# Third expert layer of a decoder: token parts of 12, 12 and 8 tiles in place of 8, 12 and 12, with the first part's scatters sent four at a time

## What is computed

```
def _L3_ffn_ref(x, keys, w1, b1, w2, b2, rw, rb):
    E, TOP_K = (16, 4)
    diff = x[:, :, None, :] - keys
    dist2 = jnp.sum(diff * diff, axis=-1)
    logits = -dist2 + jnp.einsum('bld,ed->ble', x, rw) + rb
    topv, topi = jax.lax.top_k(logits, TOP_K)
    w = jax.nn.softmax(topv, axis=-1)
    hidden = jax.nn.gelu(jnp.einsum('bld,efd->blef', x, w1) + b1, approximate=False)
    exp_out = jnp.einsum('blef,edf->bled', hidden, w2) + b2
    sel = jnp.take_along_axis(exp_out, topi[..., None], axis=2)
    fused = jnp.sum(w[..., None] * sel, axis=2)
    return fused
...
    x = _layernorm(x + _L3_xattn_ref(x, ctx_512, ...), axis=-1)
    x = _layernorm(x + _L3_ffn_ref(x, L3_ffn_keys, ...), axis=-1)
```

## Time and profile before

| what | value |
|---|---|
| median of 3 runs | 4205.87 us (4192.5 to 4210.88) |
| the profiled execution: its time | 4187.43 us |
| its span, first to last instruction | 4185.6 us |
| mean granted TensorE clock | 0.868 of full speed |
| PE busy | 3230.9 us, 77% of the span |
| DVE, ACT, POOL busy | 2781.3, 2066.4, 1179.1 us |

### The profile page before, as it was taken

How to read it: one execution, slowest core, us unless ns; L and a number is a source line. 1 busy time by engine, 2 the same in 40 slices (tenths; PEclk the granted TensorE clock), 3 DMA queues, 4 the chain that set the end, 5 groups by cost and what they waited for, 6 DMA issues and landing times. The chain is left out here.

```text
span 4185.6 us, 91928 instructions
## 1 busy us (share of the span) xinstructions
PE 3230.9 (77%) x33262; PEld 2232.8 (53%) x33262; DVE 2781.3 (66%) x7659; ACT 2066.4 (49%) x4648; POOL 1179.1 (28%) x2276
## 2 busy tenths in 40 slices
PE   6886888796888776857898989668865588779881
PEld 2443555463555446854555555345544456569881
DVE  5884677374787584547787888577754668844453
ACT  3664666223443543535786878445640344346551
POOL 2322221012110233451111111253312520334555
PEclk9987999697998687977999999688985699889996
DMA  4424331033220431231212121423430500222332
GB/s 94 67 34 61 57 53 36 16 98 50 32 38 11 62 69 57 79 69 35 50 27 42 36 38 30 67 35 65 60 79 11 172 20 1 77 68 88 90 84 62
DMA packets 321466, 232.56 MB, mean 56 GB/s; under 512 B 46253, under 2 KB 305946, under 8 KB 320838
## 3 DMA queue, kind: packets, MB, share of 16 engines
q1 hardware_dynamic: 307226, 199.40, 23.5%
q0 software_dynamic: 12928, 26.50, 2.2%
q10 hardware_dynamic: 864, 0.79, 0.1%
HBM read 69.21 MB, written 55.63 MB: 30 GB/s over the span
## 5 line engine op out<-in xcount | busy, mean ns | idle before, releaser
L1412 ACT ACTIVATE PT<-ps 128x512 f32<-128x512 f32 (+1 forms) x1600 | 812.1, 560 | 338.4 <-PE ps L1348 247.6
L1362 DVE TENSOR_REDUCE M<-ps 128x2 f32<-128x512 f32 x1024 | 653.0, 684 | 127.1 <-PE ps L1348 104.0
L1314 PE MATMUL ps<-SKB 51*128 51x256 bf16 (+3 forms) x3584 | 415.7, 276 | 133.2 <-DVE M L1362 67.2
L1359 DVE TENSOR_REDUCE M<-ps 128x3 f32<-128x384 f32 x768 | 390.2, 550 | 148.4 <-PE ps L1348 90.6
L1505 PE MATMUL ps<-PT,VA 128*9 128x256 f32 (+1 forms) x7168 | 454.2, 373 | 1.3 <-ACT PT L1412 1.0
L3857 ACT ACTIVATE SKB<-ps,SKB 128x128 f32<-128x128 f32 x1032 | 295.5, 372 | 273.8 <-PE ps L3775 192.4
L1452 PE MATMUL ps<-SKB 53*128 53x256 bf16 (+3 forms) x3584 | 358.5, 268 | 46.9 <-DMA SKB<-MT 36.2
L1348 PE MATMUL ps<-tri,idh 64*128 64x128 bf16 x5120 | 392.6, 222 | 0.0
L3921 DVE COPY SKB<-SKB 128x1028 f32 (+1 forms) x258 | 186.7, 724 | 283.2 <-PE ps L3784 162.7
L1314 PEld LDWEIGHTS ps<-SKB 51*128 51x128 bf16 (+1 forms) x3584 | 131.9, 96 | 403.4 <-DVE M L1362 157.1
L3784 PE MATMUL ps<-SKB 128*128 128x128 f32 x2064 | 287.1, 284 | 23.3 <-ACT SKB L3857 18.6
(11 more groups left out here) (496 smaller groups left out, 6289.7 us busy)
## 6 DMA issues: line engine op xcount, KB each, us to landing
SKB<-HH SPq DMA_DIRECT2D x1212, 64.0 KB
SKB<-HH SPq DMA_DIRECT2D x576, 32.0 KB
PT<-L_sorted_rows SPq DMA_DIRECT2D x258, 64.0 KB
L_sorted_results<-SKB SPq DMA_DIRECT2D x258, 64.0 KB
SKB<-in_L3f_w SPq DMA_DIRECT2D x32, 256.0 KB
L_sorted_rows<-TV SPq DMA_DIRECT2D x2, 4032.0 KB, 28.5
SKB<-scratch SPq DMA_DIRECT2D x2, 2048.0 KB, 11.7
SKB<-in_L1f_w SPq DMA_DIRECT2D x16, 256.0 KB
```

The costliest lines, as they stand in the source:

```text
L1314: k = e.matmul(self.mx_bank(m + i)[:, o:o + n], K.QS[self.set(c)][64 * i:64 * i + rows, s, 256 * bb + 128 * qt:256 * bb + 128 * qt + 128], ...
L1359: k = e.tensor_reduce(K.M3[n % 2][:, hh, 0:3], mx[:, 0:384].rearrange("p (a k) -> p a k", a=3), axis=AX.X, op=ALU.max)
L1362: k = e.tensor_reduce(K.M3[n % 2][:, hh, 0:2], mx.rearrange("p (a k) -> p a k", a=2), axis=AX.X, op=ALU.max)
L1412: e.activation(K.PT[:, x % 4, n * i:n * i + n], self.st_bank(x, i)[:, 0:n], ACT.Exp, bias=0.0, scale=self.scale).then_inc(*self.exp.inc())
```

## The change

Three numbers of the part split change, and with them the slots in which the gates of the parts begin (13 and 25 before, 17 and 29 after). `each` becomes 4, and within such a group of four the scatters don't wait for each other. The sums inside the block loop become those of all chunks ahead of the last part, 24 in place of 20.

```
-        split, most = ((0, 8), (8, 12), (20, 12)), 12
+        most = max(tiles for _, tiles in split)
...
     def pool_first(self, e):
         for i in range(self.D.parts[0].tiles * self.top):
             if i > 0 and i % self.each == 0:
                 yield
-            if i > 0 and not self.alone:
+            if i > 0 and not self.alone and (self.each == 1 or i % self.each == 0):
                 e.wait_ge(self.scattered[0].sem, self.scattered[0].base + 16 * i)
             self.pool_scatter(e, 0, i)
...
-        s, early = 0, 5 * self.top
+        late = self.D.parts[2].chunks[0]
+        s, early = 0, late * self.top
...
-        for c, slots in ((5, (0, 16)), (6, (16, 29)), (7, (29, 32))):
-            self.follow(self.next and self.next.dve_lead, e, *slots)
+        for c in range(late, 8):
+            self.follow(self.next and self.next.dve_lead, e, *{5: (0, 16), 6: (16, 29), 7: (29, 32)}[c])
             while s < (c + 1) * self.top:
                 self.dve_sum(e, s)
                 s += 1
...
-        g5 = ChosenGates(K, s4, W[5], 8, "L1", 2, Room([K.SKB[:, 0:6096]]), Room([K.GG[:, :]]), None)
+        g5 = ChosenGates(K, s4, W[5], 8, "L1", 2, Room([K.SKB[:, 0:6096]]), Room([K.GG[:, :]]), None, ((0, 8), (8, 12), (20, 12)))
...
-        g12 = ChosenGates(K, s11, W[12], 16, "L3", 4, room, room, K.HH[0][:, :, :].rearrange("p a b -> p (a b)"))
-        s12 = ChosenExperts(K, s11, W[12], g12, ("L3f_w1", "L3f_w2", "L3f_b1"), ACT.Gelu, 0, at=(13, 25), rate=(3, 4), each=2, own=1,
+        g12 = ChosenGates(K, s11, W[12], 16, "L3", 4, room, room, K.HH[0][:, :, :].rearrange("p a b -> p (a b)"),
+                          ((0, 12), (12, 12), (24, 8)))
+        s12 = ChosenExperts(K, s11, W[12], g12, ("L3f_w1", "L3f_w2", "L3f_b1"), ACT.Gelu, 0, at=(17, 29), rate=(3, 4), each=4, own=1,
                             last=True)
```

More of the change, by code:

```diff
@@ L3291, with __init__ @@
 class ChosenGates:
-    def __init__(self, K, ahead, W, E, kind, top, room, late, hot):
+    def __init__(self, K, ahead, W, E, kind, top, room, late, hot, split):
         self.K, self.ahead, self.W, self.E, self.kind, self.top = K, ahead, W, E, kind, top
         self.pitch = 1028 + 2 * (kind == "L1")
-        split, most = ((0, 8), (8, 12), (20, 12)), 12
+        most = max(tiles for _, tiles in split)
         self.wide = [room.take(most * E) for _ in range(5 + top + (2 if top > 2 else 1))]
```

## The result

The changed kernel takes 4185.91 us (median of 18 runs, 4172.5 to 4197.21), against 4204.78 us for 18 runs of the kernel before on the same chip: a ratio of 0.9948, 95% interval 0.9938 to 0.9959. The forecast was 4187.4 us. Its profiled execution took 4186.57 us with a span of 4184.8.

The account below looks back on a forecast made before the run. PE was taken to pace the blocks, gathers the tail, and scatter waits the start and first border. Terms -23.3 + 7.9 - 5.3 - 1.7 - 3 + 7 gave -18.4 us, so 4187.4 us against the median; range 4170 to 4204.

Parts of the forecast that it names:

- tail: Behind the last stored block: two chunks of POOL's gathers in place of three, -23.3 us, nearly sure.
- loop, 99 to 172: Blocks 99 to 172: a sixth chunk gathered and summed inside the loop costs +7.9 us, bounds 4 and 15.7.
- first border: Border of parts 0 and 1: part 1's scatters land before they are needed, -5.3 us, lower bound 3.5.
- gates: blocks 0-3: Loop's start: PE does 16 small matmuls for the last part's gates in place of 24, -1.7 us.
- gates: blocks 3-28: Blocks 2 to 28: DVE's gate operations 128 columns wide in place of 192, -3 us (0 to -4).
- start: Ahead of the first block: 48 scatters in place of 32 bring it later, +7 us (bounds +2 and +16).
- the prediction's own last sentence: Signs of error: loop's chunk cost not constant, lighter DVE slots not moving cross-attention's end, grouped scatters over 1.3 us each.
- Block 95's burst: Blocks 95 to 99, eight gathers back to back: 15.45 us in place of 7.6, the loop term's upper bound.
- A: Rival: the first block's start doesn't move, +1 in place of +7, loop at 6; sum -26 us, 4179.5 us; chance 0.30.
- B: Rival: the block loop takes back the tail's gain, added chunk 15.7 us; sum -10.6 or -7.6; chance 0.21 with D.
- C: Rival: scatters without waits slow down ahead of the first block, start +54, sum +29 us; chance 0.05.
- D: Rival: remaining waits grow with four scatters in flight; start +16, sum -9.4, 4196.5 us; chance 0.21 with B.

Follow-up runs that it names:

- first pair: The first profiles of the kernel before and the changed kernel, ahead of the later sets; the runs' medians were 4204.78 and 4185.91 us, ratio 0.9948.
- c2: The kernel before, unchanged, profiled once more beside the follow-up runs: 4143.57 us.
- c1: The changed kernel itself, run again beside the follow-up runs: 4118.47 us, ratio 0.9935 to the kernel before.
- e3: The changed kernel with 20 sums inside the block loop in place of 24, chunk 5's behind it: 4123.08 us, ratio 0.9944 to the kernel before.
- set 3: One of four later sets of runs, each on another chip; its runs of the kernel before had a median of 4197.71 us.
- e4: The changed kernel with 16 sums inside the block loop, chunks 4 and 5 behind it: 4144.7 us, ratio 0.9994 to the kernel before.
- e1: The changed kernel with each of part 0's 48 scatters again waiting for the one ahead: 4170.73 us, ratio 1.006 to the kernel before.
- e6: The changed kernel with eight result buffers in place of four in the last stage: 4115.26 us, ratio 0.993 to the kernel before.
- e5: The changed kernel with five scatters to a slot and no wait among part 0's: 4108.4 us, ratio 0.991 to the kernel before.

## Why the prediction was right, and where only its sum was

The total, -18.4 us, met the first pair's -18.1, and that it met it so closely is luck: the terms below don't agree as well, and where the loop is undisturbed the same change is worth 28.2 us. Its terms, in us:

```
                      predicted   first pair   c2 to c1
tail                   -23.3       -23.3        -23.1
loop, 99 to 172         +7.9       +13.9         +5.9
first border            -5.3        -5.3         -5.4
gates: blocks 0-3       -1.7        -2.6         -2.6
gates: blocks 3-28      -3          -5.7         -6.1
start                   +7          +1.9         +3.1
73-77 and 95-99          0          +3.0          0
```

- **Tail and first border** came out at the forecast. Chunks of POOL's gathers are back to back, so one less is 23.3 us less. Blocks 47 and 48 follow in 1.90 us each, without the 3.46 us wait of the earlier trace rows. The rest of the border's 5.3 us is PE's busy time, 5.78 us there before and 3.80 after, at a granted clock of 0.81 and 1.00; the prediction doesn't name it. What I hadn't seen is that the tail's term holds two edits, 14.2 us from the part of chunk 5 and 8.9 us from its sums (e3).
- **Loop.** The term was right in kind and wrong in its base. I divided 39.7 us by five chunks, and 15.5 us of it were chunks (c2), the rest a disturbance that is in the first pair and in set 3 and not in the others. An added chunk costs 5.6 to 5.9 us undisturbed, 2.4 us of it a pause of PE and the rest two more falls of the clock (c1 and c2). By the prediction's own last sentence it is wrong if the cost per chunk isn't constant; it isn't: the fifth costs 1.3 us and the sixth 5.6 (e4, e3, e1). In the first pair the sixth cost 13.9, inside my bounds but not at my value. Block 95's burst, which I had used as the dear end for eight gathers, costs nothing undisturbed.
- **Gates of the last part.** Mis-sized, -8.3 measured against -4.7. The 16 small matmuls took 3.51 us as reckoned (it is the row L3361 above). Blocks 0 to 3 take 10.9 us in e1 and e6, where the granted clock there is 0.50 as before the change, so 1.9 of the 2.6 us are the lighter gates and the rest the clock (0.59 in the changed kernel). Blocks 3 to 28 gave 5.7 us and not 3, beyond my upper bound of 4. The term held DVE's lighter operations alone, and PE's idle time in that stretch fits it, 7.8 us before and 5.2 after. The other 3.1 us are PE's busy time, at a granted clock of 0.96 before and 1.00 after. The stretch before, and after:

```profile
3696.69:3762.66 65.97, 58.17 (x464) 54.97 (x463) 45.03 (x129) 38.69 (x135) 26.18 (x26) 0.96 0.25 76
3713.36:3773.64 60.28, 55.09 (x462) 52.25 (x462) 40.84 (x128) 37.96 (x134) 25.62 (x25) 1.00 0.28 82
```

  c2 and c1 show the same, 0.96 and 1.00. What raised the clock wasn't tested.
- **Start.** The chain behind the last root was right: 3698.98 - 3676.45 = 22.5 us, against 22.8. The step that failed is the one ahead of it, that the last root would come where it came before. It comes 4.7 us earlier, 3672.42 - 3412.0 = 260.4 us behind the first reduce against 265.1. All nine waits that the trace shows among the 48 scatters sum to 14.5 us, one of 3.50 and the others of some 1.53 or less, and the cross-attention's last reduce came 6.9 us earlier where I had taken 4. So the start lost 1.9 us in place of 7.
- **The rivals.** A (the start moves by 1 us, the loop takes 6, the sum is -26) was nearer than the forecast on the start, wrong on the first pair's sum, and nearer than the forecast to the undisturbed pair's -28.2. B's mechanism, the loop takes back the tail's gain, is partly what the first pair shows, 13.9 of the 15.7 us that it gave, but that the cause is store or load landings that grow with the gathers isn't shown: with six chunks the undisturbed loop is only 5.9 us longer, and e6 didn't run where the loop was disturbed. C falls: the median scatter takes 967 ns in the changed kernel, and of this stage's 128 the 50 that overlap one of DVE's 128x1028 copies have a median of 965 ns and a longest of 1404, with up to 20 in a row without a wait in e5. The rule of the Trainium skill, SBUF — State Buffer, "SBUF: two separate sides", doesn't show for these copies and these scatters. D falls too: of the waits behind four in flight only that first one was long. Whether it moved the last root isn't shown: DVE's operation that the root waits for (L489) was done at 3672.33 us and POOL's last scatter ahead of it at 3672.36.

Right and wrong terms cancelled: start and gates gave 8.7 us more than forecast, loop and the stretches beside it took 9.0 more. By the stages of one profile each, the change is worth more where the loop isn't disturbed, 28.2 us against 18.1. The ratios of the runs lean the same way, 0.9935 and 0.9948, but their intervals overlap.

## What to carry to other kernels

A chain of indirect scatters that wait for each other costs twice their issue time (2.51 against 1.27 us), and where a later part's first block hangs on the chain's end, the waits are the first thing to take out, before the work is split anew; but such a chain also blocks what is queued behind it, so more to a slot isn't always better (five gained, six lost it again). When work moves from a tail into a loop, look for the longest unbroken piece that it puts on one engine of the loop and for the pause that this makes in the engine that sets the pace (2.1 to 2.6 us a chunk here), and cut that piece to fit the turn. Then look at the granted clock behind the pause: where it fell, the same place cost 3.7 to 4.5 us. A term read from a stretch's length alone holds both. And before a stretch's excess is divided by what one thinks causes it, look at the same stretch in another profile of the same code, from another chip if there is one: 24 of the 39.7 us here weren't the chunks'.

## What the runs showed of the hardware that was not expected

The loop took 153 to 160 us in three sets and 178 to 192 in the first pair and set 3. The granted clock of the whole execution is the same (0.866 and 0.868 of full speed in c2 and before), and that of blocks 99 to 172 nearly so, 0.98 and 0.96: PE is busy for 142.89 and 152.87 us of them, so 10.0 of the 24.5 us between these two are busy time and the rest idle time. How much of the busy time is the clock's wasn't separated. In before's first trace, ScalarE's waits in blocks 99 to 172 are put down to no engine of the core ("remote") for 14.7 + 6.6 us, and those of DVE's weight copies for 28.6 us; in c2 no such wait shows in this stretch. Waits of ScalarE before, 3921 to 4100, and then in c2, 3902 to 4056 (total us, times, longest):

```profile
ACT SKB L3857 <- PE ps L3775: 45.7, 46, 3.8
ACT SKB L3857 <- remote: 14.7, 8, 2.5
ACT SKB L3857 <- issue: 8.9, 9, 4.0
ACT SKB L3865 <- remote: 6.6, 8, 1.4
```

```profile
ACT SKB L3857 <- PE ps L3775: 57.0, 73, 4.1
ACT SKB L3865 <- PE ps L3784: 0.9, 2, 0.4
```

In before's trace the semaphore that TensorE sets at the end of a block's matmuls was recorded more than 0.1 us behind the (modelled) end of the matmul for 77 of 148 of them between 3905 and 4090 us, and by 1.2 us on average. In c2 none of 155 was. This evidence is weak, since records are missing in before's trace: from 3905 to 4090 us it has 62 updates for 74 blocks' second matmuls (L3784), and from 3815 to 3900, where the blocks keep their full pace, 20 for 44. A lost record looks like a late one, and a wait whose record is lost can be put down to "remote". The disturbance begins with the gathers (block 95) and in part at block 73. Whether TensorE itself or the path of its semaphores is late, and why only in some sets, stays open: no experiment here could switch it on or off.
